# A two-layer graph network in one launch: the second node pass from feature-major x, its sums in TensorE, and row statistics in a PSUM bank

## The reference

```
h = relu(layernorm(x))
# layer 0
score = sum(h[src] * h[dst]); a = softmax of score over each dst
agg = segment_sum((h @ W_conv + b_conv)[src] * a)
out = agg + relu(h @ W_res + b_res)
x2 = x + batchnorm(out)                # mean and variance over all nodes
# layer 1
h2 = relu(layernorm(x2))
msg = gelu(gelu([h2[src], h2[dst], edge] @ W_m1 + b_m1) @ W_m2 + b_m2)
boxes = segment_sum(msg over dst)
c = gelu([h2, boxes] @ W_c1 + b_c1)
result = x2 + h2 + gelu(c @ W_c2 + b_c2)
```

## Time and profile before

| | us |
|---|---|
| median of 3 runs (lowest, highest) | 1620.09 (1619.15, 1623.63) |
| profiled execution, its span | 1614.88, 1613.1 |
| busy: TensorE, VectorE, ScalarE, GpSimd | 1254, 1377, 833, 1250 |
| mean granted TensorE clock | 0.857 |

### The profile page before, as it was taken

The page is one execution under the profiler, slowest core; times in us unless marked ns, Lnnn a source line. Parts: engine busy times, 40 slices in busy tenths (PEclk is TensorE's granted clock), DMA queues, the critical chain, the costliest instruction groups (busy, mean ns, idle before and its releaser), DMA issues.

```text
span 1613.1 us, 21823 instructions
## 1 busy us (share of the span) xinstructions
PE 1254.2 (78%) x6521; PEld 842.9 (52%) x6521; DVE 1376.9 (85%) x2302; ACT 832.7 (52%) x1448; POOL 1250.2 (78%) x1062
## 2 busy tenths in 40 slices
PE   3566777776667567598899898898679998999992
PEld 1355666565555455376676666666444433434440
DVE  8899899999887788698989888888279987999991
ACT  4555545454544244476676676675225444454541
POOL 7777777777777777788888777786777678877776
PEclk9778878797887788688988897898579998999996
DMA  7688877454544335344554555653477544655510
GB/s 212 231 302 322 288 252 261 146 172 153 170 133 157 95 112 184 142 146 174 201 191 175 180 193 189 201 184 125 145 171 167 145 128 118 145 146 136 132 41 19
DMA packets 132612, 273.54 MB, mean 170 GB/s; under 512 B 30404, under 2 KB 47658, under 8 KB 132496
## 3 DMA queue, kind: packets, MB, share of 16 engines
q1 hardware_dynamic: 76004, 187.38, 34.2%
q0 software_dynamic: 39360, 43.42, 12.9%
q10 hardware_dynamic: 17132, 41.35, 7.0%
HBM read 151.68 MB, written 121.80 MB: 170 GB/s over the span
## 4 chain that ended last, share of the span: by engine, by line
POOL 31%; DVE 28%; issue 19%; PE 13%; DMA 4%; ACT 3%; DVEq 0%; SPq 0%; POOLq 0%; ACTq 0%
POOL agg_rows L605 12%; POOL part L601 6%; DVE stat L760 4%; DVE stat L768 4%; POOL out L605 4%; PE banks L1490 3%; POOL agg_ring L601 3%; DVE sq L1032 3%; DVE part L774 2%; DVE sums L1006 2%; POOL gout L601 2%; POOL x_ring L601 2%; DMA edge_agg<-agg_ring 2%; PE banks L1480 2%; PE banks L1374 2%
## 5 line engine op out<-in xcount | busy, mean ns | idle before, releaser
L601 POOL DMA_INDIRECT agg_ring<-agg_rows,edge_idx x196 | 233.7, 1192 | 82.8 <-issue 55.9
L605 POOL DMA_INDIRECT agg_rows<-agg,put_first x196 | 234.4, 1196 | 58.0 <-issue 56.2
L605 POOL DMA_INDIRECT out<-agg,put_last x196 | 221.7, 1131 | 59.8 <-issue 59.5
L601 POOL DMA_INDIRECT part<-in_x,edge_idx x192 | 218.9, 1140 | 58.5 <-issue 57.6
L1490 PEld LDWEIGHTS banks<-packed,cT 97*128 97x128 f32 (+1 forms) x1568 | 214.7, 222 | 42.6 <-issue 42.4
L1359 PE MATMUL banks<-ident,xc 128*128 128x128 f32 (+1 forms) x784 | 136.1, 323 | 129.4 <-DVE xc L774 128.7
L1490 PE MATMUL banks<-packed,cT 97*128 97x64 f32 (+1 forms) x1568 | 223.0, 307 | 0.0
L1359 PEld LDWEIGHTS banks<-ident,xc 128*128 128x128 f32 (+1 forms) x784 | 112.4, 176 | 139.6 <-DVE xc L774 118.9
L1480 PE MATMUL banks<-hT,packed 64*96 64x512 f32 (+1 forms) x392 | 122.5, 702 | 55.8 <-ACT cT L1214 52.3
L1097 ACT ACTIVATE hT<-banks 128x512 f32<-128x512 f32 (+1 forms) x98 | 55.3, 595 | 198.3 <-PE banks L1359 197.2
L601 POOL DMA_INDIRECT x_ring<-in_x,edge_idx x104 | 122.0, 1173 | 34.3 <-issue 34.0
(11 more groups left out here) (165 smaller groups left out, 3007.0 us busy)
## 6 DMA issues: line engine op xcount, KB each, us to landing
xt<-in_x SPq DMA_DIRECT2D x84, 512.0 KB, 5.7
r_rows<-rT ACTq DMA_DIRECT2D x48, 512.0 KB, 4.6
agg_rows<-rb SPq DMA_DIRECT2D x48, 512.0 KB
out<-xt SPq DMA_DIRECT2D x36, 512.0 KB, 2.8
edge_r<-rr ACTq DMA_DIRECT2D x48, 256.0 KB, 3.8
rT<-r_rows SPq DMA_DIRECT2D x24, 512.0 KB, 6.9
part<-r_rows SPq DMA_DIRECT2D x24, 512.0 KB, 6.4
rr<-edge_r SPq DMA_DIRECT2D x48, 256.0 KB, 3.3
```

The costliest lines, as they stand in the source:

```text
L601: A.indirect_dma_start(to, None, table[:, :], bass.IndirectOffsetOnAxis(ap=idx, axis=0), bounds_check=limit, oob_is_err=False).then_inc(si ...
L605: A.indirect_dma_start(table[:, :], bass.IndirectOffsetOnAxis(ap=idx, axis=0), rows_of, None, bounds_check=limit, oob_is_err=False).then_i ...
```

## The change

Stored beside x is a feature-major copy of it (`in_x_t`, laid out like r, made before the launch; the transposition of the input is not in the launch). In the second pass

- VectorE adds normalised r and x feature-major (`make_x2`), two steps ahead; nothing is transposed back first.
- TensorE centers and turns to rows in one product with the matrix I - 1/64 within each feature block (`center_x2`, banks 0 to 3); ScalarE squares out of PSUM; VectorE scales out of PSUM into a ring `hx` of 5 (`scale_h2`).
- The out product is feature-major: two products of 512 columns per half step instead of eight of 64, both halves into bank 7. Transposes of h2 go through bank 4, c products to banks 5 and 6.
- x2 and the out rows come back to rows as a sum in PSUM, 16 products with the identity a step (`sum_back`), two pairs later; VectorE adds h2 to that (`final_rows`). Neither GpSimd nor VectorE adds h2 otherwise.

GpSimd puts all groups, then gathers 43 of 49 groups of `gather_agg` in one go, into a ring of 8 that SyncE empties by a schedule of its own; 6 are left for the edge stage. In the joint stage row sums and final inverse deviations are in bank 5 (`row_stat`), so weighted rows are transposed through bank 4 alone; the edge stage keeps `stat`.

```diff
-RS = 4
+RS = 8
+HS = 5
...
+        def agg_gathered(i):
+            return max(0, min(G - 6, 3 * i - 30))
...
-            for s in range(S):
-                if s % 2 == 0:
-                    add_h2(s)
-                for n in range(agg_groups(s - 1), agg_groups(s)):
-                    if is_group(n):
-                        put_agg(n)
-                    if n == G:
-                        G_p.all_done(pool, G)
-                    if is_group(n - G):
-                        gather_agg(n - G)
-            ahead = agg_groups(S - 1) - G
+            for n in range(PUTS_AHEAD, G):
+                put_agg(n)
+            G_p.all_done(pool, G)
+            ahead = G - 6
             last = G - ahead
+            E_ctr.done(pool, G - 1)
...
+            def node_stat(i, s, p):
+                return row_stat[0:p, i * P + (s % 2) * R:i * P + (s % 2 + 1) * R]
...
-                subtract_mean(xc[s % CS][0:p, :], xt[s % XS][0:p, :], dstat(0, s, p), A_ctr, s, 1)
+                subtract_mean(xc[s % CS][0:p, :], xt[s % XS][0:p, :], node_stat(0, s, p), A_ctr, s, 1)
...
-                                     bank(4 + n % 2)[0:D + 1, 0:c][:, ::-1], carry,
+                                     bank(4)[0:D + 1, 0:c][:, ::-1], carry,
...
+                             in_stage(N_inv, t_), row_stat[:, P + c0:P + c1])
...
-            def x2_center(s):
-                p = nodes_of(s)
-                here = xb[s % XB][0:p, :]
+            def make_x2(s):
+                p = nodes_of(s)
+                here = blocks(xb[s % XB][:, :], p)
                 dve.wait_ge(B_x.of(s), B_x.after(s))
-                dve.wait_ge(B_rt.sem, B_rt.after(s))
-                V.tensor_tensor(here, W[0][0:p, :], here, ALU.add).then_inc(B_f.sem, 1)
-                dve.wait_ge(B_f.sem, B_f.after(s, 1))
-                B_t.done(dve, s - CS)
-                h2_added(dve, s - CS)
-                B_sq.done(dve, s - 2)
-                subtract_mean(xc[s % CS][0:p, :], here, dstat(0, s, p), B_f, s, 2)
...
-                V.tensor_tensor(here, here, xc[s % CS][0:p, :], ALU.add).then_inc(B_yv.sem, 1)
+                dve.wait_ge(B_rb.sem, B_rb.after(s))
+                V.tensor_tensor(here, here, blocks(rb[s % 2][:, :], p), ALU.add).then_inc(B_f.sem, 1)
+
+            def scale_h2(s):
+                p = nodes_of(s)
+                B_st.done(dve, s - HS)
+                relu_scale(rows(hx[s % HS][0:p, :]), rows(W[s % 2][0:p, :]), dstat(3, s, p), B_h)
...
+                here = hx[s % HS][0:p, :]
+                dve.wait_ge(B_bk.sem, B_bk.after(s))
+                V.tensor_tensor(here, W[s % 2][0:p, :], here, ALU.add).then_inc(B_fin.sem, 1)
...
-                if a in pair:
-                    x2_center(a)
-                if is_step(a - 1):
-                    add_h2_here(a - 1)
-                if is_step(a - 3):
-                    final_rows(a - 3)
-                if b in pair:
-                    x2_center(b)
-                if a in pair:
-                    p = nodes_of(a)
-                    sum_squares(dstat(1, a, p), sq[0][0:p, :], B_sq, a, B_ss)
-                if b in pair:
-                    sum_squares(dstat(1, b, P), sq[1][:, :], B_sq, b, B_ss)
-                if is_step(a - 2):
-                    final_rows(a - 2)
+                for s in (a, b):
+                    if is_step(s - 4):
+                        final_rows(s - 4)
+                    if is_step(s + 2):
+                        make_x2(s + 2)
...
+                A.activation(sq[s % 2][0:p, :], W[s % 2][0:p, :], ACT.Square).then_inc(B_sq.sem, 1)
...
-                A.activation(gout[s % 2][0:p, c], bank(6 + b)[0:p, :], ACT.Gelu).then_inc(B_og.sem, 1)
+                B_bk.done(act, s - 2)
+                A.activation(blocks(gout[s % 2][:, c], p), blocks(bank(7), p), ACT.Gelu, bias=bc2[:, :])\
+                 .then_inc(B_og.sem, 1)
...
-                E_scan.done(pe, n - 2)
+                E_scan.done(pe, n - 1)
...
-                for n in edges:
-                    if is_group(n - 2):
-                        transpose_weighted(n - 2)
+                if is_group(edges[0] - 2):
+                    transpose_weighted(edges[0] - 2)
...
+                    if n == edges[0] and is_group(n - 1):
+                        transpose_weighted(n - 1)
...
-            def transpose_r(s):
-                p = nodes_of(s)
-                pe.wait_ge(B_rb.sem, B_rb.after(s))
-                B_f.part(pe, s - 1, 1)
+            def center_x2(s):
+                p = nodes_of(s)
+                pe.wait_ge(B_f.sem, B_f.after(s))
+                if s < 4:
+                    B_h.done(pe, s - 2)
+                B_fin.done(pe, s - 4)
...
-                    ins = T.transpose(W[0][0:p, k * P:(k + 1) * P], rb[s % 2][:, k * P:k * P + p], ident[:, :])
-                ins.then_inc(B_rt.sem, 1)
+                    ins = T.matmul(W[s % 2][0:p, k * P:(k + 1) * P], xb[s % XB][:, k * P:k * P + p], cen[:, :],
+                                   start=(k % 4 == 0), stop=(k % 4 == 3))
+                ins.then_inc(B_cen.sem, 1)
...
+                if b:
+                    pe.wait_ge(B_ht.sem, B_ht.after(s, 1))
+                else:
+                    B_ht.done(pe, s - 1)
+                for i in range(4):
+                    c = (4 * b + i) * P
+                    ins = T.transpose(bank(4)[:, i * P:i * P + p], hx[s % HS][0:p, c:c + P], ident[0:p, 0:p])
...
-                to = bank(6 + b)
                 pe.wait_ge(B_cg.sem, B_cg.after(s, b + 1))
-                B_og.part(pe, s - 1, b + 1)
-                for i in range(8):
-                    ins = T.matmul(to[0:p, i * D:i * D + D], cT[b][:, i % 2, (i // 2) * P:(i // 2) * P + p],
-                                   wc2[:, :], start=(i == 0), stop=(i == 7))
+                if b:
+                    pe.wait_ge(B_og.sem, B_og.after(s, 1))
+                else:
+                    B_og.done(pe, s - 1)
+                for i in range(2):
+                    ins = T.matmul(blocks(bank(7)[i * D:i * D + D, :], p), wc2[0:H2, :], blocks(cT[b][0:H2, i, :], p),
+                                   start=True, stop=True)
                 ins.then_inc(B_o.sem, 1)
 
-            transpose_r(0)
-            for i in range(PAIRS + 1):
+            def sum_back(s):
+                p = nodes_of(s)
+                if is_step(s + 2):
+                    pe.wait_ge(B_h.sem, B_h.after(s + 2))
+                else:
+                    B_fin.done(pe, s - 2)
+                B_og.done(pe, s)
+                for k in range(K):
+                    to = W[s % 2][0:p, k * P:(k + 1) * P]
+                    T.matmul(to, xb[s % XB][:, k * P:k * P + p], ident[:, :], start=(k % 4 == 0), stop=False)
+                    ins = T.matmul(to, gout[s % 2][:, k * P:k * P + p], ident[:, :], start=False, stop=(k % 4 == 3))
+                ins.then_inc(B_bk.sem, 1)
```

More of the change, by code:

```diff
@@ L186, in program @@
         ec = [part[2 + q // 2][:, (q % 2) * EC:(q % 2 + 1) * EC] for q in range(4)]
-        esq = [sb(f"esq{q}", [P, EC]) for q in range(2)]
+        esq_pair = sb("esq_pair", [P, 2 * EC])
+        esq = [esq_pair[:, q * EC:(q + 1) * EC] for q in range(2)]
         rr = [sb(f"rr{q}", [P, EC]) for q in range(6)]
@@ L192, in program @@
         sums = [sb(f"sums{q}", [D + 1, EG]) for q in range(2)]
-        heT = [sb(f"heT{q}", [P, EG]) for q in range(2)]
+        heT_pair = sb("heT_pair", [P, 2 * EG])
+        heT = [heT_pair[:, q * EG:(q + 1) * EG] for q in range(2)]
+        hx = [esq_pair, xc[0], xc[1], xc[2], heT_pair]
         inv = [sb(f"inv{q}", [P, EJ]) for q in range(2)]
@@ L221, in program @@
         bank_sum = bank(3)
+        row_stat = bank(5)
         s_w = sem("weights_loaded")
@@ L277, in program @@
         B_rb = stage("r_normed")
[L278 to L279 removed]
+        B_f = stage("x2_made")
+        B_cen = stage("x2_centered")
         B_sq = stage("x2_squared")
@@ L291, in program @@
         B_og = stage("out_gelu", 2)
+        B_bk = stage("x2_and_out_rows_summed")
         B_fin = stage("final_row_ready")
@@ L542, in _ @@
                 load_rows(s)
-            for s in range(2, RB):
+            for s in range(2, RB + 2):
                 load_r(s)
@@ L546, in _ @@
                 a = 2 * i
-                for s in (a + RB, a + RB + 1):
+                for s in (a + RB + 2, a + RB + 3):
                     if is_step(s):
                         load_r(s)
+                for s in (a + 4, a + 5):
+                    if s >= XB and is_step(s):
+                        load_rows(s)
                 if i == PAIRS - 1:
@@ L735, in setup_weights @@
                                   cols(bias_part[32 * i:32 * i + 1, i, :], K)).then_inc(s_b, 1)
+                V.memset(cen[:, :], 0.0).then_inc(s_b, 1)
+                dve.wait_ge(s_b, 9)
+                for q in range(2):
+                    V.memset(cen[q * D:q * D + D, q * D:q * D + D], -1.0 / D).then_inc(s_b, 1)
+                dve.wait_ge(s_b, 11)
```

(7 more changed lines are left out.)

156 lines of the change are left out of this document (82 added, 74 removed).

## The result

| | before | after |
|---|---|---|
| median of 4 runs (lowest, highest), us | 1620.19 (1619.15, 1623.63) | 1779.63 (1773.75, 1784.88) |
| span of the profiled execution, us | 1613.1 | 1778.9 |
| joint stage, second pass, edge stage, us | 646.2, 513.5, 453.4 | 671.8, 660.4, 446.7 |

The ratio is 1.098, with an interval of 1.094 to 1.102: the changed kernel is slower by 160 us. The forecast was 1725, with a range up to 1790.

A forecast was written before the change was run, and what follows sets the result against it. VectorE was taken to bound the joint stage, TensorE the second pass, both the edge stage. +16 + 111 - 22 = +105 on 1614.9 gave 1720, with some 5 for timed runs 1725 us; range 1620 to 1790.

The forecast's parts named there:

- my own case: Whole kernel: forecast of 1725 us with waits at banks 4 and 7, spanning 1670 to 1780; chance 0.70.
- the rival with the low clock: Second pass: waits pull TensorE's clock down, about +4 us a pair, +90, 1815 us in all; chance 0.12.
- Gathers: Joint stage: GpSimd's gathers come down to 1.00 us and VectorE's 31.8 us of waits for them go.
- Statistics in PSUM: Joint stage: row sums and inverse deviations in a PSUM bank cost VectorE 0, at the upper end +17 us.
- Scan wait: Joint stage: VectorE's second scan waits 2.15 us a round for the second group's transposes; +48 us, bounds +12 and +83.
- Joint stage: Whole joint stage: scan wait of 48 us less 32 us of gather waits, +16 us.
- The pair of the second pass: Two steps of the second pass: 20.6 us of TensorE products plus waits at bank 7, 25.0 us.
- the clock: Second pass: TensorE priced at the higher clock, 22 pairs at 25.0 us, 550 us.
- Second pass: Whole second pass: 625 us against 513.5, +111.
- Edge stage: Two parts: TensorE's waits for GpSimd's accumulating load shrink by 12 us, the scatter tail by 10; -22, bounds 0 and -26.
- the one without waits: Second pass: no waits behind banks 4 and 7, TensorE at 20.6 us a pair, 1623 us; chance 0.10.
- The one by way of GpSimd: Gather waits go, second scan needn't wait, pairs below about 20.5 us: 1575 us; chance 0.08.

The follow-up runs named there:

- the last version: Kernel before plus statistics in PSUM, one bank, weighted-row transposes ahead of the r product, all h2 additions on VectorE: 1581.55 us, ratio 0.978.
- the joint stage's repair: Changed kernel with second-pass waits filled and, as this repair, second group's weighted rows transposed ahead of the first group's edge product: 1644.98 us, ratio 1.012.

## Why the prediction was right, and where it was off

The direction and most of the mechanisms held, the size was 55 us short (+160 against +105). The 1780 us lie at the upper edge of the 1670 to 1780 that I gave my own case, nearer to the rival with the low clock (1815) than to my 1725; they are inside the range because the range was wide. By its terms:

- Gathers: the 32 us of waits go. They did; mean 1.008 us instead of 1.140 in the largest group. In the changed kernel the longer rounds could have done it as well, but the last version has none of these waits with rounds of 23.1 us.
- Statistics in PSUM: 0, with +17 as a bound. Within 1 us it was 0: the reduction of a step (L768, xt) takes 1211 ns into PSUM and 1203 into SBUF in the joint stage, the small one 683 against 677. The scalings read the statistics at no cost that the trace shows (L774, xc: 1208 ns from PSUM, 1212 from SBUF). The Trainium skill's "VectorE: DVE Perf Modes" (The TRN2 errata) gives a PSUM source the larger fixed cost, 120 cycles against 58; this case's traces show no such difference, and leaving it out of the sum was right.
- Scan wait: +48 forecast from 2.15 us a round, 56.9 measured in 24 waits. Mechanism and place were right. I had taken the round at 245 for all; in the changed kernel rounds with 1.9 and 3.0 us mostly take turns, the 3.0 where the r product runs at the lower clock for longer. Joint stage: +16 forecast, +25.6 measured.
- The pair of the second pass: 25.0 forecast, 25.2 measured at full clock. Counted as the forecast counts, the waits are 4.2 instead of 4.4 and the products 21.0 instead of 20.6: a sum back takes 3.67 us and not 3.56, a centering 1.89 and not 1.78.
- **The step that failed in size is the clock.** I took the 25.0 for all pairs because the pair of the edge stage in the earlier trace rows kept 1.00, and gave the low clock a rival of its own that doubles the second half (+4 a pair). What happened lies between: dips in 15 of 22 pairs, 26.2 us on the mean. That is 27 us over 22 pairs, 5 of it from 25.2 for 25.0. Filling or shortening the first wait removed the dips in every pair that ran without a stop. The start of the stage lost to the lower clock too, there behind idle times of 8.1 and 5.6 us: to the first sum back it took 38.3 us and not 32, with the first 32 instructions of centering at 6.60 us instead of 3.56. Second pass: +111 forecast, +147 measured.
- Edge stage: -22 forecast, -6.7 measured. The first part was right: TensorE's waits for the accumulating load fell from 26.7 to 13.4 us. The second was not: 10 us of the tail were to go, and none did. From VectorE's last instruction to the last scatter's start it is 19.6 us (1751.6 to 1771.2) and was 19.5, because in both the last groups are finished close together and their scatters stand in one row at the end. Some 5 us were given back in the stage's first groups, where TensorE's granted clock was 0.70 (30 to 60 us into the stage) and had been 0.98; this was not tested.

Of the rivals, the one without waits (1623) fell: the waits are there, and filled they give 1645 only together with the joint stage's repair. The one by way of GpSimd (1575) fell too: it needed pairs of 20.6 us and a scan that doesn't wait, and of its three parts only the 32 us of gathers came. The one with the low clock (1815) fell in its size; its mechanism is a part of what happened.

## What to carry to other kernels

Price a move of work from an engine with room to the one that sets the pace at the full sum of its products, and add the waits, for a buffer that has lost its double or for work that shorter products no longer hide: here TensorE got 6.0 us more of work (21.5 busy against 15.5 in an undisturbed pair) and 3.7 us of waits ahead of the out products, in a pair of steps that had taken 17 to 22. Before giving up such a change, look at what can stand in the waits: the same products in another order were 99 us faster in that stage, though still 47.5 slower than the old ones. And where a bank goes from two to one, put the writer right behind its reader's release, since what stands between is paid once a round: the scan's waits were 56.9, 18.3 and 1.3 us as less stood between.

## What the runs showed of the hardware

- With waits of 1.56, 0.77 and 1.36 us in each pair of some 25 us, TensorE was at its lower clock for a stretch in 15 of 22 pairs; with 0.43 in place of the 1.56 and the other two kept, no dip was seen in ten pairs, and with 0.43 as the only wait none in 22.
- Gathers of GpSimd (the largest group) took 1.07 to 1.14 us on the mean in the four traces with the row statistics in SBUF, and 1.00 to 1.01 in the ten with them in PSUM, with the same instructions of VectorE at nearly the same lengths (1239 and 1225 ns for the subtraction over 1024 columns).
